# Graph attention scores: keys placed ahead of the spreading of the digits, and a spreading product over two rows

## What is computed

```
    e_s = jnp.einsum('nho,ho->nh', h, a_src)
    e_d = jnp.einsum('nho,ho->nh', h, a_dst)
    scores = jax.nn.leaky_relu(e_s[edge_src] + e_d[edge_dst], NEG_SLOPE)
    m = jax.ops.segment_max(scores, edge_dst, num_segments=N)
```

## Time and profile before

| | |
|---|---|
| median of 3 runs | 2746.41 us (2726.57 to 2752.91) |
| the profiled execution | 2740.57 us |
| its span | 2738.8 us |
| busy: PE, DVE, POOL, ACT | 61%, 60%, 53%, 30% |
| granted clock of TensorE, mean | 0.80 of full |

### The profile page before, as it was taken

How to read it: one execution, slowest core, us unless ns; L and a number is a source line. 1 busy time by engine, 2 the same in 40 slices (tenths; PEclk the granted TensorE clock), 3 DMA queues, 4 the chain that set the end, 5 groups by cost and what they waited for, 6 DMA issues and landing times. The chain is left out here.

```text
span 2738.8 us, 38544 instructions
## 1 busy us (share of the span) xinstructions
PE 1679.5 (61%) x9983; PEld 1342.2 (49%) x9983; DVE 1652.3 (60%) x2687; ACT 833.9 (30%) x2134; POOL 1444.6 (53%) x1557
## 2 busy tenths in 40 slices
PE   4367534677655544486655777504477767767688
PEld 4255423455543433486544566403355545545577
DVE  6455763677654545676424655796366657668675
ACT  3144210000000000465212222205355545534454
POOL 3655676655656664526155555477665655530050
PEclk8599857788876776588777999856689888878899
DMA  4535544555423333344152545454555555331010
GB/s 137 183 101 159 178 140 123 170 174 157 120 81 92 95 92 106 112 142 131 51 175 81 163 154 160 161 190 128 157 166 170 172 164 158 106 101 32 4 43 31
DMA packets 132988, 346.47 MB, mean 127 GB/s; under 512 B 39881, under 2 KB 66521, under 8 KB 119347
## 3 DMA queue, kind: packets, MB, share of 16 engines
q0 software_dynamic: 66144, 180.94, 23.5%
q1 hardware_dynamic: 63407, 158.51, 16.5%
q10 hardware_dynamic: 3364, 6.16, 0.7%
HBM read 262.24 MB, written 83.28 MB: 126 GB/s over the span
## 5 line engine op out<-in xcount | busy, mean ns | idle before, releaser
L1366 PE MATMUL ms_ps_m<-ms_msg,ms_pick 128*128 128x260 f32 x1408 | 415.6, 458 | 287.1 <-issue 199.8
L892 POOL DMA_INDIRECT e_ring<-table,e_index x465 | 442.6, 952 | 252.2 <-issue 137.6
L1347 DVE TENSOR_TENSOR ms_msg<-e_ring,ms_ps_w 128x1040 f32<-128x1040 f32 (+1 forms) x352 | 436.6, 1240 | 141.8 <-issue 128.0
L1366 PEld LDWEIGHTS ms_ps_m<-ms_msg,ms_pick 128*128 128x128 f32 x1408 | 313.0, 229 | 389.7 <-issue 332.2
L1366 PE MATMUL ms_ps_m<-ms_msg,all_xn 128*128 128x272 f32 x1408 | 386.0, 437 | 191.5 <-issue 167.1
L892 POOL DMA_INDIRECT e_ring<-table,l_index x369 | 353.9, 959 | 227.3 <-issue 111.1
L1366 PEld LDWEIGHTS ms_ps_m<-ms_msg,all_xn 128*128 128x128 f32 x1408 | 290.0, 212 | 287.3 <-issue 218.9
L767 PE MATMUL sc_ps_e<-sc_keys,sc_hot 125*128 125x100 bf16 (+1 forms) x3840 | 322.7, 241 | 168.6 <-DVE all_xn L712 141.7
L767 PEld LDWEIGHTS sc_ps_e<-sc_keys,sc_hot 125*128 125x128 bf16 x3840 | 276.8, 104 | 238.8 <-issue 123.4
L934 POOL DMA_INDIRECT w_staged<-table,l_stage_index x256 | 257.3, 1005 | 183.5 <-issue 66.9
L670 ACT ACTIVATE sc_rows<-sc_ps_b 125x512 bf16<-125x512 f32 x320 | 171.2, 598 | 433.6 <-PE sc_ps_b L755 251.8
(11 more groups left out here) (513 smaller groups left out, 2743.3 us busy)
## 6 DMA issues: line engine op xcount, KB each, us to landing
ahead<-w_staged SPq DMA_DIRECT2D x32, 1056.0 KB
e_ring<-ahead SPq DMA_DIRECT2D x32, 1056.0 KB
ahead<-e_ring SPq DMA_DIRECT2D x20, 1040.0 KB
e_ring<-ahead SPq DMA_DIRECT2D x20, 1040.0 KB
e_ring<-table,e_index POOLq DMA_INDIRECT x465
all_acc<-ahead SPq DMA_DIRECT2D x27, 256.0 KB
ahead<-all_acc SPq DMA_DIRECT2D x27, 256.0 KB
e_ring<-table,l_index POOLq DMA_INDIRECT x369
```

What stands on the lines that cost most here:

```text
L892: pool.indirect_dma_start(out=g.ring[:, slot * QUAD + i // GT, i % GT, :], out_offset=None, in_=s.table[:, :], in_offset=bass.IndirectOffs ...
L1347: dve.tensor_tensor(msg[:, b, :, 0:R].rearrange("p t (h o) -> p t h o", h=H), ring[:, bass.ds(slot, 1), :, :].rearrange("p a t (h o) -> p ...
L1366: mm = pe.matmul(ps_m[b][:, 0:W], pick[:, b, t, :], msg[:, b, t, :], start=t == 0, stop=t == GT - 1)
```

## The change

The keys are placed first: on PE the 44 placing products now stand ahead of the spreading of the first four items, and on DVE the pieces of `band` ahead of `which`. The fill of `pair` with zeros is gone, with the semaphore `pair_zero` and ACT's wait for it. The spread product now reads rows 0 and 1 alone, of `which` and of `pair`, in both layers and for every item.

```
-            act.wait_ge(pair_zero, 1)
...
-            dve.memset(pair[:, :, :, :], 0.0).then_inc(pair_zero, 1)
-            dve.tensor_scalar(which[:, :], s.lane_row[:, :], LOW - 0.5, s.node_of[:, 0:1], ALU.is_ge, ALU.is_equal).then_inc(which_set, 1)
             dve.memset(band[:, 0:P], 0.0).then_inc(band_set, 1)
             dve.memset(band[:, 2 * P:3 * P], 0.0).then_inc(band_set, 1)
             dve.tensor_copy(band[:, P:2 * P], s.ident[:, :]).then_inc(band_set, 1)
+            dve.tensor_scalar(which[0:2, :], s.lane_row[0:2, :], LOW - 0.5, s.node_of[0:2, 0:1], ALU.is_ge, ALU.is_equal).then_inc(which_set, 1)
...
-                    pe.matmul(ps_b[(2 * i + half) % 4][:, :], which[:, :], b[:, i, half * HALF:(half + 1) * HALF],
+                    pe.matmul(ps_b[(2 * i + half) % 4][:, :], which[0:2, :], b[0:2, i, half * HALF:(half + 1) * HALF],
                               start=True, stop=True).then_inc(spread, 1)
...
-            pe.wait_ge(which_set, 1)
-            for q in range(lanes):
-                spread_ids(q, pair[:, q // 2, :, :], q % 2, q < 2)
             pe.wait_ge(band_set, 3)
             for hi in range(HI):
...
             mm.then_inc(moved, 1)
+            pe.wait_ge(which_set, 1)
+            for q in range(lanes):
+                spread_ids(q, pair[:, q // 2, :, :], q % 2, q < 2)
             pe.wait_ge(keys_ready, -(-HI // BANK_HI))
```

More of the change, by code:

```diff
@@ L614, in edge_scores @@
         pair_in = m.sem("pair_in")
-        spread, rows_kept, pair_zero, which_set = (m.sem(n) for n in ("spread", "rows_kept", "pair_zero", "which_set"))
+        spread, rows_kept, which_set = (m.sem(n) for n in ("spread", "rows_kept", "which_set"))
         hot_ready, looked, picked = m.sem("hot_ready"), m.sem("looked"), between.picked
```

## The result

The changed kernel took 2781.6 us (median of three runs, 2776.6 to 2794.1) against 2746.4 before: ratio 1.015, 95% interval 1.010 to 1.020. It is slower by 35 us where 9 us less were forecast, and lies outside the range of 2711 to 2761. The profiled execution has a span of 2779.9 us against 2738.8, so 41 us are to be found.

A forecast was written before the change was run, and what follows sets the result against it. No engine was taken as full; POOL and the look-ups hold each other. Gains of 7.2 us in stage one and 1.8 in stage two sum to 9.0, taking the median from 2746.41 to 2737.4 us, range 2711 to 2761.

The forecast's parts named there:

- What bounds the kernel: Both score stages: no engine is full; POOL and the look-ups hold each other, so the smaller gain counts.
- The fill and the loads: Stage starts: one MEMSET of 1.76 us goes per stage; in stage one all four first loads issue 2.0 us earlier.
- The order on PE and the hole: Stage starts: placing products end 9.4 and 5.8 us earlier; holes of 10.7 and 2.9 us before the cast move along.
- the full gain: Rival, stage starts: no hole remains, look-ups start 15.1 and 7.7 us earlier, 22.8 together, 2724 us; chance 0.12.
- POOL's gain of 7.2 us: Stage one: POOL's first scatter starts at 112.6 instead of 119.80; counted as smaller than the look-ups' 9.4 us.
- The products over two rows: All 320 spread products: rows fall from 128 to 2, columns stay, so no time is gained or lost.
- The rival "slower": Both score stages: two-row products switch PE's setting, 320 changes at 0.15 us, 48 us, 2785 us; chance 0.12.
- The clock: Both score stages: the granted clock could fall with less of the array working; given no time of its own.
- The test that was named: Stage one: prediction wrong if it ends under 4 or over 12 us earlier, or its 5.0 us cycle changes.
- The rival "swallowed": Stage starts: POOL's gather runs hold back PE's signals, so only the loads move, 2746 us; chance 0.26.

The follow-up runs named there:

- e5_after: The changed kernel itself, unaltered, on a chip of the follow-up experiments; 2370.1 us, ratio 1.0251 to the kernel before.
- e7: Changed kernel plus, ahead of each pair of two-row products, two overwritten products over 128 rows and 384 columns; 2300.0 us, ratio 0.9935 to before.
- e3: Changed kernel with the zero fill kept behind the band and spread products over 64 rows instead of 2; 2316.0 us, ratio 0.9971 to before.
- e9_before: The kernel before, unchanged, run against itself on a chip of the experiments; ratio 1.0001.
- e12: Changed kernel plus, ahead of each pair of two-row products, two overwritten products over 128 rows and 128 columns; 2386.7 us, ratio 1.0322 to before.
- e14: The kernel before with spread products over two rows in the second score stage alone, old order and fill kept; ratio 0.9970 to before.

## Why the prediction was wrong, point by point

*What bounds the kernel: right for the chip of the profile.* Its messages began 72.1 us behind the end of the stage, so a microsecond of the stage did count.

*The fill and the loads: right for the first two loads only.* They are issued at 70.26, as forecast near 70.0, and the fill is gone. But the third goes at 78.50 and the fourth at 83.40, where 80.0 was forecast and 82.03 stood before: ACT took the first spread product at 77.70, 3.1 us behind its start at 74.58 (before: 75.08 and 74.46), and the later loads stand behind that work in its program and behind the landing of the load before.

*The order on PE and the hole: half right.* The placing products come first. The forecast kept a hole of 10.7 us and put the cast near 85; it came at 77.07, 2.4 us behind the end of the products at 74.64. That was the case of the full gain ("under 80"), but PE's first look-up came at 84.41 and not at the 80.0 of that rival, since it waited for the late loads. In the second stage the cast came 9.5 us behind the last split of the scores (1440.46 less 1431.0) instead of 16.4 (1409.57 in the earlier trace rows, less 1393.2): 6.9 us gained where 5.8 were forecast. From the timeline of after:

```profile
1440.46 0.85 DVE L734 CAST sc_keys<-sc_ps_e 100x504 bf16<-100x504 f32 x2 [5.49 <-remote]
```

*POOL's gain of 7.2 us: wrong in sign.* POOL's own part came as forecast: its 17th gather started at 91.45 (92.1 forecast) and its 32nd ended at 111.14 (112.3). The step "with the cast at 85.2 that is 110.4, before POOL asks" took over the 25.2 us that DVE needed from the cast to the first edges; that work now took 46.0 us (77.07 to 123.05), and POOL waited 11.9 us for it. The near flags of DVE, 40 instructions of one line and 40 reads behind them, first in before, then in after, then in e5_after on another chip (busy, mean ns, idle before):

```profile
L582 DVE TENSOR_SCALAR_CACHE_REDUCE sc_near_flag<-all_acc,all_node_of 128x250 bf16<-128x250 int32 x40 | 16.3, 469 | 4.8 <-DVE sc_near_flag L582 3.2 <-issue 1.5
```

```profile
L582 DVE TENSOR_SCALAR_CACHE_REDUCE sc_near_flag<-all_acc,all_node_of 128x250 bf16<-128x250 int32 x40 | 16.9, 470 | 13.0 <-issue 9.1 <-DVE sc_near_flag L582 4.0
L582 DVE DVE_READ_ACCUMULATOR sc_near_flag<-all_acc,all_node_of 128x1 f32 x40 | 3.3, 83 | 10.5 <-issue 10.5
```

```profile
L582 DVE TENSOR_SCALAR_CACHE_REDUCE sc_near_flag<-all_acc,all_node_of 128x250 bf16<-128x250 int32 x40 | 15.8, 470 | 0.0
L582 DVE DVE_READ_ACCUMULATOR sc_near_flag<-all_acc,all_node_of 128x1 f32 x40 | 3.4, 84 | 0.0
```

In after that is 23.5 us of idle time (13.0 and 10.5) inside a chain that waits for nobody. The rows show when it comes: from 86.0 us, 15 us into POOL's run of gathers, until 116.3, 5 us behind its end. POOL, then DVE, in after:

```profile
91.45 0.95 POOL L932 DMA_INDIRECT e_ring<-table,e_stage_index  x1 [0.30 <-issue]
...
110.19 0.95 POOL L932 DMA_INDIRECT e_ring<-table,e_stage_index  x1 [0.30 <-issue]
...
86.85 0.47 DVE L582 TENSOR_SCALAR_CACHE_REDUCE sc_near_flag<-all_acc,all_node_of 128x250 bf16<-128x250 int32 x1 [0.79 <-DVE sc_near_flag L582]
...
114.15 0.47 DVE L582 TENSOR_SCALAR_CACHE_REDUCE sc_near_flag<-all_acc,all_node_of 128x250 bf16<-128x250 int32 x1 [1.31 <-issue]
```

In before the chain ran under gathers as well, but POOL's wait of 3.45 us at the 17th gather had cut them into two runs: in the second, from 95.29, DVE's delays began only at 109.0, when most of the chain was done, and the hole behind the placing products (from 83.9) lies in the same late part of the first, from 70.78. The change took that wait away and made one run of 40 us out of two, from 71.31 to 111.14. So the saved wait of POOL was paid for on DVE. That a long unbroken run of gathers causes the delays is read from these three places, not tested, and on the other chips it does not happen: e5_after has the same unbroken run (62.47 to 102.43) and no idle time in the chain.

*The products over two rows: the step that failed.* "Time does not follow the rows there, so I take nothing" read the price of a product by itself, and that stayed: at 2.4 GHz two spread products are recorded as 0.60 us together in e7, 0.61 before. What changed lay beside it: the clock of the whole stage, for which the forecast had no term, and the changes of setting. The rival "slower" priced the change of setting at 0.15 us, 48 us in all and 2785 us, with a chance of 0.12. The result, 2781.6, lies there, which is luck. The size of a change was about right (0.09 to 0.10 us at 2.4 GHz; at 1.2 GHz the starts in after are 562 and 218 ns apart at the two changes, against 427 and 82 ns at that clock before, so 0.135), but it was not the mechanism that made the loss: e3 has every one of these changes at a clock of 0.99 and is not slower.

*The clock: the other half of that step, dismissed with a wrong reason.* "I give this no time of its own, because 24 look-up products an item over 125 rows stay as they were." They did stay, and the clock fell all the same, from 0.90 to 0.50. The working of an item would have shown the stakes. In after it is 23 gaps of 82 ns between look-ups, then 218, 400 and 562 ns: 3.07 us, as measured. With the changes of setting but the high clock, e3 shows 1.71 us (140.81 to 142.52), less than the 2.5 us an item that POOL and the signals allowed before. So on that chip too the switch alone should have been hidden. With the low clock but no changes of setting an item would take 3.07 less 2 x 0.135, or 2.80 us, which is above 2.5: the fall of the clock alone makes PE the bound, and the changes add to it once it is. (Both are estimates from these rows; neither was run on that chip.) From the third item on, 0.57 us an item over 78 items is 44 us, and the stage lost 40 there.

*The test that was named did its work.* "The prediction would be wrong … if the cycle of 5.0 us in the middle of the stage changes at all": two items now take 6.14.

*Chances.* The rivals held 0.12 for a slower kernel, with a warning from two sides, the setting and the clock. What should have raised it is that two separate mechanisms had no row that spoke against them, while the whole gain to be weighed against them was 9 us.

## What to carry to other kernels

A product over few rows costs its own time, two changes of setting, and possibly the clock of everything around it. Zero rows that only seem to waste the array can be what keeps a stage at 2.4 GHz. Before thinning out one kind of product in a dense stage, work out what the whole stage takes at 1.2 GHz and whether PE would then be its bound; and where a small gain is forecast at the start of a stage, look for the next engine that is full (here POOL up to 316 us), because it decides whether any of it arrives. When a wait is removed, look also at what it kept apart: a chain that is moved, or a run of gathers that no longer stops, meets other neighbours, and its length has to be read again there (here 25.2 us became 46.0).

## What the runs showed of the hardware that was not expected

The clock step: with spread products over 2, 32 and 33 rows the granted clock of the first stage was 0.50, with 64, 65 and 128 rows 0.99 (0.96 in e9_before, which starts later). The same two-row products stood at a clock of 0.99 in e7, at 0.50 in e12 and e5, and at 1.00 in the second stage of e14. Why 33 and 64 rows differ is not shown by these runs.

The change of setting from and to the look-ups over 125 rows costs 0.09 to 0.10 us at a clock of 0.99 and 0.135 at 0.50. Spread products over 64 rows and fewer pay it, those over 65 and 128 rows don't.

Chips differ: the same program took 2746 us on the chip of the first profile and 2311 to 2321 on four others. (That it is the chip, and not another condition of that pair, is not shown.) In the first stage of that profile POOL was kept waiting by PE for 49.0 us, here 3.5 (groups by line, before and e9_before, 60 to 330 us):

```profile
L934 POOL DMA_INDIRECT e_ring<-table,e_stage_index x135 | 131.3, 973 | 87.2 <-PE sc_ps_e L767 49.0 <-issue 30.0 <-remote 6.4
```

```profile
L934 POOL DMA_INDIRECT e_ring<-table,e_stage_index x160 | 163.1, 1019 | 48.5 <-issue 43.3 <-PE sc_ps_e L767 3.5 <-DMA e_ring<-table,e_stage_index 0.9
```

The hole of 10.73 us between the last placing product and the cast of the keys is 0.1 us in e9_before (the last placing product ends at 76.03, the cast starts at 76.14). On the chip of the first profile the instructions of DVE, ACT and PE come late while POOL makes a long run of gathers, most of all in its later part, as the near flags above show; on the others they don't. The rival "swallowed" of the prediction saw this, but took it for a delay of PE's signals alone. Why the chips differ in this is open.
